# Row maxima of the third and fourth attention: four matmuls of 32 rows in place of zero-padded ones of 128, and maxima ordered block by block

## What is computed

```python
# third (L2): causal, 512 rows of context, 16 heads of 16
q = (x @ Wq + bq).reshape(B, T, H, D).transpose(0, 2, 1, 3)
k, v = jnp.split(context @ Wkv + bkv, 2, axis=-1)      # to heads as q
att = jnp.einsum('bhtd,bhsd->bhts', q, k) * (1.0 / jnp.sqrt(D))
att = jnp.where(causal[None, None], att, -jnp.inf)
y = jnp.einsum('bhts,bhsd->bhtd', jax.nn.softmax(att, axis=-1), v)
return y.transpose(0, 2, 1, 3).reshape(B, T, C) @ Wp + bp
# fourth (L3): the same without mask and biases, 1024 rows of context,
# q and k turned by rotary tables before the product
```

## Time and profile before

| | before |
|---|---|
| median of 3 runs | 2950.0 us (2949.27 to 2957.69) |
| profiled execution | 2951.47 us, its span 2949.7 us |
| mean granted TensorE clock | 0.883 of 2.4 GHz |
| TensorE busy (matmuls) | 2375.2 us, 81% of the span |
| VectorE busy | 1576.8 us, 53% |
| ScalarE, GpSimd busy | 907.5 us (31%), 948.3 us (32%) |
| L1184 (row maxima matmuls) | 384 matmuls, 171.8 us busy, mean 517 ns |
| L1363 (fourth attention's reduces) | 256, 159.2 us busy, mean 684 ns |

### The profile page before, as it was taken

The page is one execution under the profiler, slowest core; times in us unless marked ns, Lnnn a source line. Parts: engine busy times, 40 slices in busy tenths (PEclk is TensorE's granted clock), DMA queues, the critical chain, the costliest instruction groups (busy, mean ns, idle before and its releaser), DMA issues.

```text
span 2949.7 us, 31683 instructions
## 1 busy us (share of the span) xinstructions
PE 2375.2 (81%) x11832; PEld 1668.5 (57%) x11832; DVE 1576.8 (53%) x2705; ACT 907.5 (31%) x1752; POOL 948.3 (32%) x817
## 2 busy tenths in 40 slices
PE   3799999848968999996885777399788989659994
PEld 2455555528955555553874454289644444348884
DVE  5788888743145665653315766322477767421222
ACT  2454555412124444442112223000224444401111
POOL 2354554433332342333222211355400000044443
PEclk8899999959978999997897777599879999769997
DMA  3000000008930000000482321199522221048883
GB/s 119 1 9 10 18 10 10 1 33 310 316 128 1 0 10 9 1 1 15 157 273 71 80 65 50 48 318 327 164 57 69 59 62 45 17 170 298 300 296 116
DMA packets 103178, 298.08 MB, mean 101 GB/s; under 512 B 16913, under 2 KB 45841, under 8 KB 102641
## 3 DMA queue, kind: packets, MB, share of 16 engines
q0 software_dynamic: 45168, 206.99, 20.3%
q1 hardware_dynamic: 57856, 89.07, 10.2%
HBM read 244.22 MB, written 20.32 MB: 90 GB/s over the span
## 4 chain that ended last, share of the span: by engine, by line
PE 41%; DVE 12%; issue 7%; DMA 4%; POOL 2%; ACT 2%; SPq 0%; another core or an unknown queue 0%; DVEq 0%; POOLq 0%; ACTq 0%
PE psum L1860 8%; PE psum L275 7%; PE psum L1883 6%; PE psum L1211 3%; DVE plain L1363 3%; PE psum L1224 2%; PE psum L646 2%; DMA plain<-in_l_en,plain 2%; PE psum L1184 2%; PE psum L661 2%; DVE plain L1381 2%; DMA plain<-sorted_x 2%; DVE plain L1360 1%; PE psum L1250 1%; PE psum L664 1%
## 5 line engine op out<-in xcount | busy, mean ns | idle before, releaser
L275 PE MATMUL psum<-split 128*128 128x512 f32 (+1 forms) x1776 | 475.3, 416 | 57.1 <-DVE split L348 11.1
L1860 PE MATMUL psum<-plain 128*128 128x128 f32 x3904 | 494.4, 279 | 10.2 <-DMA plain<-in_l_shared 8.5
L1860 PEld LDWEIGHTS psum<-plain 128*128 128x128 f32 x3904 | 486.3, 196 | 22.3 <-issue 10.5
L275 PEld LDWEIGHTS psum<-split 128*128 128x128 f32 x1776 | 337.0, 208 | 191.8 <-issue 95.7
L1009 POOL TENSOR_TENSOR plain<-plain 128x1024 f32<-128x1024 f32 x144 | 363.5, 2524 | 239.8 <-DVE plain L807 195.9
L1984 POOL DMA_INDIRECT plain<-in_l_ffn,plain x274 | 259.8, 948 | 401.7 <-PE psum L1883 378.7
L948 ACT ACTIVATE plain<-psum 128x512 f32<-128x512 f32 x448 | 251.4, 595 | 310.5 <-PE psum L664 145.2
L1883 PE MATMUL psum<-plain 128*128 128x256 f32 x1160 | 304.2, 385 | 28.0 <-DVE plain L1949 25.5
L1480 ACT ACTIVATE plain<-psum 128x512 f32<-128x512 f32 (+3 forms) x384 | 185.8, 542 | 228.7 <-PE psum L1224 227.6
L646 PE MATMUL psum<-plain 128*64 128x512 f32 x896 | 236.9, 616 | 5.6 <-DVE plain L814 5.6
L1949 DVE TENSOR_TENSOR plain<-plain,psum 128x256 f32<-128x256 f32 x198 | 81.7, 419 | 298.2 <-ACT plain L1908 266.5
(11 more groups left out here) (177 smaller groups left out, 3024.7 us busy)
## 6 DMA issues: line engine op xcount, KB each, us to landing
split<-split SPq DMA_DIRECT2D x288, 64.0 KB, 2.0
split<-split SPq DMA_DIRECT2D x96, 128.0 KB, 2.4
plain<-sorted_x SPq DMA_DIRECT2D x76, 128.0 KB
sorted_y<-plain SPq DMA_DIRECT2D x76, 128.0 KB
plain<-in_l_w SPq DMA_DIRECT2D x16, 512.0 KB
plain<-in_l_w SPq DMA_DIRECT2D x12, 640.0 KB, 3.8
plain<-in_l_ffn,plain POOLq DMA_INDIRECT x274
plain<-in_ctx SPq DMA_DIRECT2D x8, 512.0 KB, 6.1
```

Of the source, the lines that this page charges most:

```text
L275: m = t.e.matmul(out, lhs[x], rhs[y], start=(first and n == 0), stop=(last and n == 2), skip_group_check=skip)
L1860: m = t.e.matmul(K.bank(b)[:, 256 * z + P * f:256 * z + P * f + P], ws[:, f, c0:c0 + 128], xt[:, k, :], start=(f == 0 and k == 0 and z == ...
```

## The change

The zero-padded tile `QZ` goes, with its 64 copies on VectorE and the zeroing on ScalarE. The row maxima matmuls read q's high part in place: head j's 32 partitions of `QHL` against the same 32 partitions of `KHL`. Such a matmul uses the 32 array rows of group j. TensorE therefore waits for `k_hi` and `q_hi` (ScalarE's writes) and no more for `k_lo` and `q_spread` (VectorE's). Second, the loops are turned round: query block by query block, and within it half by half of the context and head by head, so that neighbouring matmuls use different row groups. Third, in the fourth attention the maxima of all heads are kept in a larger tile and joined by one reduce at the end (128 x 32 to 128 x 16) in place of four. The weights of `paced` follow the new order.

```diff
-        self.NMX = view(20304, 16)
+        self.NMX = view(20304, 32)
...
-        self.MXC = K.NMX[:, 0:8].rearrange("p (t c) -> p t c", c=2)
+        self.MXC = K.NMX.rearrange("p (t j c) -> p t j c", j=4, c=2)
-        self.QZ = rview(22016, 2048, "p (h n) -> p h n", h=4)
...
-        parts = 4 * [c for q in range(4) for c in ([(q + 1) / 7.03125] if self.causal else [0.5689, 0.5689])]
+        parts = [c for q in range(4) for c in (4 * [(q + 1) / 7.03125] if self.causal else 8 * [0.5689])]
...
     def rowmax(n):                                  # TensorE
-        t.wait_ge("k_lo", (L, n, A.rows - 2))
-        t.wait_ge("q_spread", (L, n))
-        for j in range(4):
-            for q in range(4):
-                kn = min(512, 128 * (q + 1)) if causal else 512
-                for u in range(1 if causal else 2):
+        t.wait_ge("k_hi", (L, n, A.rows - 2))
+        t.wait_ge("q_hi", (L, n))
+        for q in range(4):
+            kn = min(512, 128 * (q + 1)) if causal else 512
+            for u in range(1 if causal else 2):
+                for j in range(4):
                     b = RB.get()
                     t.bank(b)
-                    t.e.matmul(K.bank(b)[:, 0:kn], A.QZ[:, j, 128 * q:128 * q + 128],
-                               A.KHL[0][:, 512 * u:512 * u + kn], start=True,
+                    t.e.matmul(K.bank(b)[:, 0:kn], A.QHL[0][32 * j:32 * j + 32, 128 * q:128 * q + 128],
+                               A.KHL[0][32 * j:32 * j + 32, 512 * u:512 * u + kn], start=True,
                                stop=True).then_inc(*t.up("max_mm", L, n, j, q, u))
...
     def proj(n):                                    # VectorE
         rows(n, A.rows - 1, True, 0, K.BQ[:, g:g + 1], A.QHL)
-        if n == 0:
-            v.wait_ge("q_cleared", (L,))
-        if n:
-            v.wait_ge("max_mm", (L, n - 1, 3, 3, 0 if causal else 1))
-        for j in range(4):
-            z = v.e.tensor_copy(A.QZ[32 * j:32 * j + 32, j, :], A.QHL[0][32 * j:32 * j + 32, :])
-        z.then_inc(*v.up("q_spread", L, n))
...
-                        v.e.tensor_reduce(A.MXC[:, q, u:u + 1], s, AX.X,
+                        v.e.tensor_reduce(A.MXC[:, q, j, u:u + 1], s, AX.X,
                                           ALU.max).then_inc(*v.up("row_max", L, n, j, q, u))
                     yield
-            if not causal:
-                v.wait_ge("row_max", (L, n, j, 3, 1))
-                v.e.tensor_reduce(A.NMT[:, :, 32 * j + 16], A.MXC, AX.X, ALU.max,
-                                  negate=True).then_inc(*v.up("neg_max", L, n, j))
+        if not causal:
+            v.wait_ge("row_max", (L, n, 3, 3, 1))
+            v.e.tensor_reduce(A.NMT[:, :, 16::32], A.MXC, AX.X, ALU.max, negate=True).then_inc(*v.up("neg_max", L, n))
...
     def project_values(bt):                         # ScalarE
-            zeros(K.rview(22016, 2048, "p (a n) -> p a n", n=P), 16).then_inc(*s.up("q_cleared", L))
```

More of the change, by code:

```diff
@@ L1193, in shift @@
         t.bank(b)
-        t.wait_ge(*(("row_max", (L, n, 3, 3, 0)) if causal else ("neg_max", (L, n, 3))))
+        t.wait_ge(*(("row_max", (L, n, 3, 3, 0)) if causal else ("neg_max", (L, n))))
         for i in range(4):
@@ L1348, in rowmax @@
             v.wait_ge("triangle", (L,))
-        for j in range(4):
-            v.wait_ge("neg_max", v.made["neg_max"])
-            for q in range(4):
-                for u in range(1 if causal else 2):
+        v.wait_ge("neg_max", v.made["neg_max"])
+        for q in range(4):
+            kn = 128 * (q + 1)
+            for u in range(1 if causal else 2):
+                for j in range(4):
                     v.wait_ge("max_mm", (L, n, j, q, u))
@@ L1355, in rowmax @@
                     if causal:
-                        kn = 128 * (q + 1)
                         v.e.tensor_tensor(s[:, kn - 128:kn], s[:, kn - 128:kn], A.TRI,
```

## The result

| | before | after |
|---|---|---|
| median of 4 runs each | 2949.6 us (2947.6 to 2957.7) | 2997.9 us (2994.1 to 3000.8) |
| span of the profiled execution | 2949.7 us | 2995.0 us |
| mean granted TensorE clock | 0.883 | 0.859 |
| L1184, now L1183 (row maxima matmuls) | 171.8 us busy | 155.6 us busy |

The changed kernel is slower: ratio 1.0158, 95% interval 1.0135 to 1.018. That is 48 us more, where I forecast 9 less.

What follows compares the result with a forecast made beforehand. No engine was full in the two attentions; waits to and fro between TensorE and VectorE set the end. Starts -14.3, turned order -1 and operand +6.5 sum to -8.8 us: 2950.0 becomes 2941, range 2930 to 2957.

Steps and rivals of the forecast that it cites:

- The starts: Beginnings and step 0 of third and fourth attention: row maxima no longer wait for copies; with the join, 14.3 us gained.
- The single join: Fourth attention's rowmax(0): four joins become one on four times as much, so three go; 0.6 us gained.
- The copies of later steps: nothing: Twelve removed sets of copies in later steps: VectorE waits for the selection matmul anyway, so no gain.
- The change of shape: Fourth attention's lap (one loop turn between groups of three reduces): switching from scores to 32-row row maxima costs 0.20 us.
- The new operand in the loop: a loss: Fourth attention's loop: changes between full-height and 32-row matmuls cost 1.0 us a step, +6.5 us in all.
- the clock's price there: Third attention: half a clock was said to cost little because VectorE leads; no size given.
- The rival that came true: Fourth attention's loop: 32-row matmuls lower TensorE's clock, its pieces nearly double, +60 us, about 3000; chance 0.11.
- The turned order: Third attention, six steps: scores move behind the output, covered by VectorE's larger reduces; -1 us, bounds -4 and +3.

Runs made afterwards that it cites:

- the padded kernel: The changed kernel with the zero-padded 128-row operand and its copies back, new order and single join kept: 2950.0 us, ratio 0.9979 against the kernel before.

## Why the prediction was wrong

- **The starts** were right. By the same sums 4.6 (forecast 4.5), 2.2 in step 0 of the third attention (2.2), 4.8 (4.7), 2.35 in step 0 of the fourth (2.3). The single join gave 1.0 us rather than 0.6: from the first reduce to the join's end 19.4 us against 20.4. The kernel that has 32 rows at the starts alone keeps the first gain of each attention and is 17 us faster than the kernel before.
- **The copies of later steps: nothing.** Right in the step that I read: the wait ahead of the reciprocal took up the 1.71 us of the copies, and the reciprocal starts as long after the low part as before. The kernel with all later copies is the fastest.
- **The change of shape** was right in size: 0.20 us was forecast for a lap, 4.57 in all, and 4.55 to 4.56 came in the three kernels with 64 or 32 rows.
- **The step that failed is "The new operand in the loop: a loss"**, sized at +6.5 us. It multiplied 0.20 by the laps and took for granted that the laps stay at full clock. They don't: the fourth attention spent 202 us at half clock instead of 74, and came out 48.4 us longer where starts and loop together should have made it 1 us shorter. With the 8 us that the starts and the join gained there, the new operand cost about 57 us and not 6.5. The third attention, forecast at -7.7, gave 1.1. It lost 8.7 us to the kernel that has 32 rows at its start alone (283.2 against 274.6), at a clock of 0.69 against 0.75. I had put the clock's price there at little, since VectorE leads; four other traces of the same code lie between 283.2 us at 0.69 and 288.1 at 0.66.
- **The rival that came true** is the clock's, put at about 3000 with a chance of 0.11; 2998 was measured. Its lap was 1.7 us longer at half clock by my sum, 1.95 by the trace. That its number fits so well is partly luck. It put all 35 laps at half clock, and about half of them were, which makes some 30 us and not 60. The rest came from pieces that it left out: beside the 32-row matmuls the output was busy 6.8 us longer than in the padded kernel, the projections 6.4 and the transposes 5.5. Of its two reasons, a TensorE less busy was not borne out, and few rows that count for little is still open.
- **Why I gave it so little** is the lesson. The evidence against it was the last line of the earlier trace rows: a stretch of weighing keeps 1.00. The weighing's matmuls are narrow, 32 columns of result, but read 128 rows. The row showed nothing of few rows, the very thing that the change makes. I took a likeness for a measurement, and gave too little weight to the real witness, which I had quoted: the stretch at 0.50 behind the reciprocal's wait, which showed that this attention can lose its clock.
- **The turned order** in the third attention, -1 with bounds of -4 and +3, gave -3.6 in the padded kernel (280.7 against 284.4), with the clock a little higher, 0.73 against 0.71. That is within the bounds, and two single traces don't fix it better.
- **The Trainium skill**, TensorEngine Tiling (Array Packing), section Key Properties, says that a change of tiling mode drains TensorE. The traces agree: 0.43 us from start to start at a change instead of 0.23, at full clock. It led me to look at the drain, and the time lost in drains themselves was the small part.

## What to carry to other kernels

When a change swaps full-height matmuls for row groups, ask first what clock the surrounding work has and whether it has stretches at half clock already; a zero-padded operand that looks like waste may be what holds the clock for everything beside it. Price a fall of the clock over all of TensorE's pieces on the chain, not over the edited ones. In this kernel it paid to use the small operand where another engine's preparation holds TensorE up, and the padded one in the loops. Alternating shapes matmul by matmul was the worst of all (1.0708).

## What the runs showed of the hardware

- The granted clock didn't follow TensorE's busy time: 0.92 at 87% busy, 0.78 at 90%, 0.73 at 95%; and at 0.50 it rose behind a stretch busy to 93%, and stayed there in one busy to 95%. In the fourth attention it followed the rows of the row maxima matmuls, with the other matmuls unchanged: 0.92 with 128, 0.84 with 64, 0.78 with 32 (0.75 without overlap of the groups). In the third it didn't: 0.73, 0.65, 0.69. Rows and changes of shape were never varied apart between 128 rows and fewer, so which of them lowers the clock isn't settled.
- Going between full-height matmuls and a group of 32 rows, in either direction, costs 0.20 us at full clock: 0.43 from start to start instead of 0.23. On the way from scores to row maxima the lap grew alike for 64 rows and for 32, 4.56 and 4.55 us instead of 4.37.
- Three matmuls of different row groups right behind scores overlap where their banks are free: at half clock they took 0.73 us on the chain, in one group 1.57.
- Doing more can cost less than it should: the scores twice cost 34.8 us in the padded kernel and 9.1 in the 32-row one, while the latter's clock rose from 0.78 to 0.86.
